# Four column tiles of the array for the recurrence's output and the first query's scores

## What is computed

```python
def step(h, inp):                      # state-space layer, one token
    dec, u, bt, ct = inp
    h = h * dec[:, :, None, None] + u[..., None] * bt[:, None, None, :]
    y = jnp.einsum('bhpn,bn->bhp', h, ct)
    return (h, y)

# attentions 2 and 3: how many scores of the first query are not zero
energy = jnp.einsum('bhsk,bhtk->bhst', Q, K)
lengths = jnp.sum(energy[:, :, 0, :] != 0, axis=-1)
energy = jnp.where(cols[None, None, None, :] >= lengths[:, :, None, None], -jnp.inf, energy)
```

## Time and profile before

| what | value |
|---|---|
| median of 3 runs | 1880.43 us (1878.27 to 4856.51) |
| the profiled execution's own time | 1881.97 us |
| its span, first to last instruction | 1880.1 us |
| mean granted clock of TensorE | 0.970 |
| busy: PE, PEld, DVE, ACT, POOL | 93%, 79%, 66%, 76%, 28% |

### The profile page before, as it was taken

The page is one execution under the profiler, slowest core; times in us unless marked ns, Lnnn a source line. Parts: engine busy times, 40 slices in busy tenths (PEclk is TensorE's granted clock), DMA queues, the critical chain, the costliest instruction groups (busy, mean ns, idle before and its releaser), DMA issues.

```text
span 1880.1 us, 49569 instructions
## 1 busy us (share of the span) xinstructions
PE 1753.0 (93%) x18768; PEld 1477.5 (79%) x18768; DVE 1242.2 (66%) x3163; ACT 1436.8 (76%) x4218; POOL 531.7 (28%) x1288
## 2 busy tenths in 40 slices
PE   5688999999999999999999999999999999999876
PEld 4467888888888888888888888888888888888765
DVE  2356767666777776667767666776776766767532
ACT  3256888888788888887888888788888887888753
POOL 1213233322322333323233322322332323232100
PEclk7689999999999999999999999999999999999987
DMA  6000000000000000000000000000000000000000
GB/s 242 6 7 7 10 10 2 10 10 10 10 10 10 4 8 10 10 10 10 10 10 2 10 10 10 10 10 10 2 10 10 10 10 10 7 7 2 5 4 6
DMA packets 26154, 26.58 MB, mean 14 GB/s; under 512 B 2240, under 2 KB 25024, under 8 KB 25792
## 3 DMA queue, kind: packets, MB, share of 16 engines
q1 hardware_dynamic: 25920, 23.41, 3.9%
HBM read 19.21 MB, written 4.19 MB: 12 GB/s over the span
## 4 chain that ended last, share of the span: by engine, by line
PE 79%; DVE 12%; ACT 5%; issue 3%; POOL 0%; DMA 0%; DVEq 0%; SPq 0%; ACTq 0%; POOLq 0%
PE ring L494 23%; PE ring L500 21%; PE ring L488 16%; PE score L550 6%; PE output L592 5%; PE ring L677 3%; DVE rec L1201 3%; PE output L582 2%; ACT exps L860 2%; DVE neg_max L1054 2%; PE score L541 1%; DVE res L1043 1%; DVE dx L1168 1%; ACT K L970 1%; ACT attT L872 1%
## 5 line engine op out<-in xcount | busy, mean ns | idle before, releaser
L860 ACT ACTIVATE exps<-score,neg_max 128x128 f32<-128x128 f32 x1808 | 494.1, 403 | 107.0 <-DVE neg_max L1054 107.0
L1054 DVE TENSOR_REDUCE neg_max<-score 128x4 f32<-128x512 f32 x452 | 290.0, 684 | 48.4 <-PE score L550 45.2
L1305 POOL TENSOR_TENSOR stat<-stat 128x1 f32<-128x1 f32 x224 | 129.7, 583 | 648.4 <-DVE stat L1026 637.0
L488 PE MATMUL ring<-const,exps 128*128 128x128 f32 x1808 | 256.9, 280 | 13.3 <-ACT exps L860 6.0
L866 ACT COPY weights<-ring 128x512 f32<-128x512 f32 x452 | 251.3, 596 | 9.3 <-PE ring L488 3.1
L488 PEld LDWEIGHTS ring<-const,exps 128*128 128x128 f32 x1808 | 202.4, 142 | 49.7 <-issue 26.7
L1138 DVE SCALAR_TENSOR_TENSOR conv<-raw,vectors,conv 128x128 f32<-128x128 f32 x576 | 169.1, 348 | 6.7
L494 PE MATMUL ring<-actT,w_q 128*128 128x128 f32 x1024 | 138.0, 279 | 0.9 <-ACT actT L832 0.9
L550 PE MATMUL score<-K,QB 32*128 32x128 f32 x3616 | 134.6, 282 | 1.9 <-ACT exps L860 1.7
L832 ACT COPY actT<-ring 128x256 f32<-128x256 f32 x224 | 87.4, 390 | 59.9 <-PE ring L488 57.0
L550 PEld LDWEIGHTS score<-K,QB 32*128 32x128 f32 x3616 | 113.5, 187 | 21.1 <-issue 15.6
(11 more groups left out here) (163 smaller groups left out, 3549.0 us busy)
## 6 DMA issues: line engine op xcount, KB each, us to landing
cT<-in_ctxT SPq DMA_DIRECT2D x32, 128.0 KB, 2.3
x_in<-in_x SPq DMA_DIRECT2D x32, 128.0 KB, 2.2
out<-result SPq DMA_DIRECT2D x32, 128.0 KB, 1.7
row_all<-in_rows SPq DMA_DIRECT2D x1, 1420.0 KB, 10.4
w_in<-in_in_proj SPq DMA_DIRECT2D x1, 1288.0 KB, 7.3
w_k<-in_k SPq DMA_DIRECT2D x4, 256.0 KB, 6.3
w_v<-in_v SPq DMA_DIRECT2D x4, 256.0 KB, 6.2
w_q<-in_q SPq DMA_DIRECT2D x4, 256.0 KB, 7.0
```

Source lines behind the costliest of these rows:

```text
L488: last = nc.tensor.transpose(t[:, c * P:(c + 1) * P], src[:, c * P:(c + 1) * P], ident)
L860: last = run(exps[:, n, h * P:(h + 1) * P], of, ACT.Exp, bias=neg_max[:, m, h:h + 1])
L1054: nc.vector.tensor_reduce(neg_max[:, m, 4 * half:4 * half + 4].rearrange("p (b h) -> p b h", b=each), score[:, first:first + each, 0:4 // ...
L1305: tt(stat[:, l, 10:11], stat[:, l, 2:3], stat[:, l, 4:5], ALU.pow).then_inc(S[done], 1)
```

## The change

In `Y` and in `first_scores` each matmul is divided into four: the stationary operand is cut to 32 of its 128 columns, and the output goes to the 32 partitions that belong to them. The moving operand is the same for all four. Each of the four tiles gets a semaphore (nine new ones; the fourth tile keeps the ring's `bank_full`), and the two readers on DVE wait for all of them.

```diff
@@ Y, on PE
                 for h in range(MH):
-                    last = mm(t[:, h * MD:(h + 1) * MD], decay[:, l % 2, h, :], dbx[:, l % 2, h * MD:(h + 1) * MD],
-                              start=True, stop=True)
-                last.then_inc(full, 1)
+                    for r, rows_of in enumerate(ROWS_OF):
+                        last = mm(t[rows_of, h * MD:(h + 1) * MD], decay[:, l % 2, h, rows_of], dbx[:, l % 2, h * MD:(h + 1) * MD],
+                                  start=True, stop=True)
+                        if h == MH - 1:
+                            last.then_inc(full if r == TILES - 1 else S[f"Y{r}"], 1)
@@ first_scores, on PE
                 for c in range(DC):
-                    last = mm(t[:, c * 8:c * 8 + 8], K2[:, l, c, :], q_first[:, l, c, :], start=True, stop=True)
-                last.then_inc(full, 1)
+                    for r, rows_of in enumerate(ROWS_OF):
+                        last = mm(t[rows_of, c * 8:c * 8 + 8], K2[:, l, c, rows_of], q_first[:, l, c, :], start=True, stop=True)
+                        if c == DC - 1:
+                            last.then_inc(full if r == TILES - 1 else S[f"e{a_}_{r}"], 1)
@@ gate, on DVE
                 def gate(l):
+                    for r in range(TILES - 1):
+                        dve.wait_ge(S[f"Y{r}"], nth(it, l))
                     t, read = filled(it, "Y", l)
@@ is_nonzero, on DVE
                 def is_nonzero(a_, l):
+                    for r in range(TILES - 1):
+                        dve.wait_ge(S[f"e{a_}_{r}"], nth(it, l))
                     t, read = filled(it, f"e{a_}", l)
```

More of the change, by code:

```diff
@@ L386, in decoder_stack @@
             "seed6 rstd6 x5 V4ones seed7 rstd7 x6 plus "
-            "output_read att_full0 att_full1 att_full2 att_full3 attT scores0 scores1 scores2 scores3 maxima exps").split()}
+            "output_read att_full0 att_full1 att_full2 att_full3 attT scores0 scores1 scores2 scores3 maxima exps Y0 Y1 Y2 e2_0 e2_1 e2_2 e3_0 e3_1 e3_2").split()}
         x_v = a["x"].rearrange("(i g) t d -> i t g d", g=G)
```

## The result

Over 8 executions the changed kernel has a median of 1869.7 us against 1880.68 us; one of the eight (1956.07 us, at a lower granted clock) was disturbed and is left out of the ratio, as is one of 4856.51 us of the kernel before. The ratio is 0.9937, 95% interval [0.9918, 0.9956]. A second measurement, in another run beside other kernels, gave 1864.58 us and 0.992 [0.9907, 0.9932]. The forecast was 1867 us with a range from 1857 to 1877, and within 2%.

The account below looks back on a forecast made before the run. PE, busy 93% of the span, was taken to bound the kernel. Y's net -0.44 us in 31 lanes, with e2 and e3 at 0, made -13.6 us: 1881.97 to 1868.4 us profiled, median 1867, range 1857 to 1877.

Parts of the forecast that it names:

- Y: Y's block on PE, per lane: 0.87 us of rounds plus 0.33 us, less 1.74 us removed, gives -0.54 us.
- the change of form: PE going from full array to tiles and back around Y: 0.33 us, inferred from the block of L592.
- The gate's wait: L1182 on DVE behind Y: 0.23 us more from waiting for several semaphores, bounds nothing and 0.36 us.
- rival C: Gate behind Y waits 0.36 us more, `down` late by 0.23 us; 0.3 us saved per lane, 1871 us; chance 0.14.
- Down's delay: First load of `down`, held by L1182: 0.10 us given back, leaving Y a net -0.44 us per lane.
- e3: A first_scores block in a stretch belonging to PE: 0.44 us removed, 0.11 and 0.33 us added, sum 0.00.
- e2: The first_scores block behind L550: -0.16 us itself, counted 0 because DVE sets that stretch and PE waits at L669.
- The sum: Whole kernel: -0.44 us in 31 of 32 lanes, -13.6 us; median 1867 us, 0.7% less.
- the prediction's own signs: In the profile: period 0.4 to 0.5 us shorter if right; L1182 over 0.35 us behind Y means C.
- B: Y's rounds don't shrink with the columns, a pace per record of 0.027 us: 1904 us; chance 0.09.
- E: Tiles of 64 moving columns don't run beside each other: Y takes 5.2 us, time about 1990; chance 0.02.
- D: Nothing given back at the gate and e2's time counts: 0.70 us in 32 lanes, 1858 us; chance 0.09.

Follow-up runs that it names:

- the version with one semaphore: Y in four column tiles with one semaphore raised by the last tile's last matmul, first_scores as before the change; 1858.31 us, ratio to before 0.9881.
- Y alone: Only Y in four column tiles with its four semaphores, first_scores as in the kernel before; 1866.34 us, ratio to before 0.9928.
- e2 and e3 alone: Only e2 and e3 in four column tiles with their waits on DVE, Y as in the kernel before; 1879.53 us, ratio to before 0.9999.

## Why the prediction was right, step by step

- **Y, -0.54 us expected.** From fc1 to fc2 it is 2.85 - 2.29 = 0.56 us less. A round of four tiles is as long as a stream of 64 columns, and the run with the tiles one after the other shows that they have to take turns for it. The two parts were 0.90 us for the rounds (16 of 56 ns; 0.87 expected) and 0.28 us for the change of form (0.33 expected).
- **The gate's wait, +0.23 us expected, was mis-sized.** It is 0.42 - 0.04 = 0.38 us, just over the upper bound of 0.36. That is the size of rival C, and the term of the sum that was wrong. I took the wait of a reader of four semaphores; the gate has six, and I argued that two of them, being over by then, cost nothing. In the trace L1201's 0.27 us are 0.12 us until PE has raised the last semaphore and 0.15 us for two stages of DVE's sequencer; the gate's 0.42 are the same 0.12 and 0.29 us for three stages, all of them behind the last semaphore. A semaphore that has risen long ago costs its share of a stage too.
- **Down's delay, 0.10 us expected, follows from it.** Down's load goes at the gate's start + 0.69 + 0.11, thus 0.42 + 0.80 = 1.22 us behind Y's end. The first record of `down` starts at 1.25 and not at 1.33, as I reckoned, but it is then longer: the second starts 1.54 us behind Y's end, against 1.29 in the version with one semaphore. The delay is 0.25 us. That version gets back 0.28 us per lane, and four semaphores without tiles lose 0.26. The net of Y alone is 0.30 us per lane (54.27 to 53.96) against 0.44 expected, near -0.56 + 0.25.
- **e3, 0.00 expected, and e2, 0 with -0.16 of its own.** e2 and e3 alone: ratio 0.9999, with the period 54.28 instead of 54.27 us. e3's stretch kept its 2.40 us. PE's idle in front of L669 grew by 0.22 us per lane; I had 0.15; the block of e2 itself became 0.21 us shorter, so half a change of form was too much for what tiles add behind L550.
- **The sum.** A steady lane is 0.34 us shorter, not 0.44, and by the prediction's own signs (the gate over 0.35 us behind Y, the period not 0.4 us shorter) rival C, with its 0.3 us per lane and 1871 us, describes these lanes better than the forecast. Of the 15.3 us between the profiled executions they give 8.7, and 6.5 us come from the first Y's earlier start and the first three distances, where I had counted 0.44 us per lane. That the two measurements (1869.7 and 1864.58 us) lie within 3 us of 1867 on either side is in part luck: the steady lanes gave less than I had counted and the first ones more.
- **The rivals.** B (a pace per record of 27 ns) and E (no tiles side by side) fall by the 64 records of the changed kernel in 1.04 us, 16 ns each. The Trainium skill's floor of about 25 ns between starts, "TensorE: Matmul & The Clock Gate", section "Wait — 56ns, not 53.3ns?", isn't seen between tiles: starts lie 6 to 7 ns apart inside a round. D falls with the run of e2 and e3 alone and with the gate. C's wait and delay are what was measured (0.38 us of wait, `down` late by 0.25).

## What to carry to other kernels

Look for matmuls whose moving operand has fewer columns than the stationary one. In this kernel the load set their pace (0.109 us a record for 64 columns), and dividing the stationary operand's columns over tiles that take turns brought it down to the stream (0.056 us a round), with two tiles as with four. The block must be long enough to pay for the change of form (0.28 us here, against 0.84 us saved; e3's block, four records before, gained nothing). Count the semaphores too. Four raises instead of one put the last 0.08 us later, and each stage of the reader's sequencer, for up to two semaphores, took 0.07 to 0.10 us; as the next `claim` of the bank waits for that reader, 0.28 us per lane were lost, and one semaphore on the last tile brought them back. Look for which stretch the saving falls in: e2's 0.2 us per lane were waited out 1 us later.

## What the hardware showed beyond what was expected

- How a wait for several semaphores is spent. The chain of the changed kernel in order of time, behind L582 (whose reader has four):

```profile
725.89 1.09 PE output L582 x31
726.98 0.03 issue
727.00 0.02 DVEq L1207
727.02 0.05 issue
727.07 0.05 DVEq L1207
727.12 0.04 issue
727.17 1.77 DVE rec L1208
```

DVE's sequencer (DVEq) takes two stages before the instruction itself. The chain starts them at 726.98, when the third tile's semaphore rises; the fourth rises 0.04 us later, and the reader starts 0.15 us behind that. One semaphore is asked for in the instruction and up to two in a stage: four are two stages, the gate's six are three, and with one there is no stage and the reader starts 0.02 us behind the raise. The order matters as well. The gate before had three semaphores and one stage, but that stage held the two old ones and was over long before Y's semaphore rose, so it cost nothing; in the changed kernel Y's last semaphore is asked for in the first of three stages. No run tries another order.

- How close raises can follow each other. The semaphores of four tiles, whose last matmuls start 6 to 7 ns apart, rise 0.043 us apart, in Y as in L582.

- Inside one tile records follow each other at the stream's pace, but when a block goes on in another tile, PE overlaps the two on its own, for about three records on either side (64 records in 3.11 us instead of 3.6).
